# The drain of a two-layer block in another order: the roots, the transposes of x1 and the last sums moved on four engines

## The chip, the cores and the metric

One core of one Trainium2 chip. The time is the device time of one execution in microseconds (us), the median of several runs; lower is better. The kernel before took 449.24 us (three runs, 449.08 to 449.36).

## What is computed

The input x has 4096 tokens (8 sequences of 512) of 256 features, all fp32. Two stages follow each other, each with a residual and a layer norm without weights:

```python
def attn(x):                                  # retention with 4 heads
    q, k = rotary(x @ Wq, x @ Wk)             # 4 heads x 64
    v = x @ Wv                                # 4 heads x 128
    o = chunk_retention(q, k, v, gamma)       # decay gamma per head, running state per sequence
    o = rmsnorm(o, gn_weight) * silu(x @ Wg)
    return o @ Wo
def ffn(x):
    wg, wu, wd = (w_int / 127 for w_int in (w_gate, w_up, w_down))   # 256 -> 768 -> 256
    return (silu(x @ wg.T) * (x @ wu.T)) @ wd.T
x1 = layernorm(x + attn(x))
x2 = layernorm(x1 + ffn(x1))                  # the output
```

## The kernel before

The tokens are cut into 32 tiles of 128 (NT = 32, four to a sequence). Five engines each run an order of their own, written out by hand, and meet at counting semaphores. A *slot* s does each stage for another tile: the projections of tile s, the retention of tile s-1, the output product `attention_out` and the sum z1 of tile s-2, the first layer norm (x1) and its transpose of tile s-3, the gate and up products of the pair that holds tile s-4, the down product and the second sum z2 of tile s-6, and the second layer norm of tile s-7. The tiles of the feed-forward stage go in pairs (256 columns): an even slot makes blocks 0 to 2 of the hidden layer for the pair, the odd slot after it blocks 3 to 5. I write (t, j) for block j of the slot NT + t, so that (2, 0) to (3, 2) are the six blocks of the last pair, tiles 30 and 31.

fp32 products are made from parts: each operand is split in a high part (fp32r, written by ScalarE) and the low rest (a subtraction), and TensorE multiplies high by high, low by high and high by low. For integer weights the low part of the weight is nothing, and two products remain.

What follows the last full slot is the *drain*, slots 32 to 40, with its own order on every engine. The diff touches only this part:

- TensorE (PE), `drain` at L628. `turn_x1` (L471) transposes x1 of a tile into the bank b_state; it waits for x1 and until the tile before has been read out of the bank. `gate_up_block` (L525) is 8 matmuls. `down` (L563) comes in three parts (0, 1, 2), 4 matmuls each; part j needs the low parts of blocks j and 3+j of the pair, and part 0 also a free bank, named by `free`.
- For each block of the hidden layer a loop runs over two engines: ScalarE (ACT) takes the silu of the gate (`gate`, L800), VectorE (DVE) multiplies by up (`hidden`, L1016), ScalarE writes the high part (`split_h`, L813), and then it takes the silu of the next block. GpSimd (POOL) subtracts to get the low part (`split_h`, L1255). There are two buffers for a block.
- The layer norms: VectorE makes the sum (`residual_1`, L1099; `residual_2`, L1118), its statistics and their moments (`moments_1`, `moments_2`), GpSimd the inverse root (`inv_std_1`, `inv_std_2`, two small operations, L1287 and L1289), VectorE the scaled difference (`norm_1`, L1038; `norm_2`, L1050). x1 of a tile then goes through TensorE (L485), ScalarE (high part, L756) and VectorE (low part, `split_x1T`, L1074) before the gate product may read it. z1 and its moments have one buffer, z2 two.
- SyncE stores each finished tile (L360); it waits for `norm_2`.

A few lines show the two kinds of wait that matter here:

```python
pe.wait_ge(x1_ready, n + 1)        # turn_x1: x1 of tile n
pe.wait_ge(x1T_split, n)           # turn_x1 in the drain: tile n-1 read out of b_state
dve.wait_ge(x2_ready, n - 1)       # residual_2: tile n-2 has been normed (two buffers of z2)
```

Of the kernel before, what the change touches and what calls it, by code (L numbers as in the profile page):

```python
# [29 lines left out]
F32 = mybir.dt.float32  # L30
F32R = mybir.dt.float32r
I32 = mybir.dt.int32
ALU = mybir.AluOpType
# [18 lines left out]
FFN_LAG = 4  # L52
# [16 lines left out]
def build_block(nc, xT, x, w_proj, w_o, gn, w_ffn, rope, out):  # L69
    tokens = x.shape[0]  # L70
    NT = tokens // P
# [4 lines left out]
    with ExitStack() as ctx:  # L76
# [200 lines left out]
        def down_bank(s, t):  # L277

            if isinstance(s, int) and s >= NT - 1:
                return b_rows[(1, 0, 1, 0, 1, 0, 1)[s - NT + 1]]  # L280
            return row_bank(t + 1, 1)

        def x1_bank(s, t):
# [89 lines left out]
        def _(pe):  # L373
# [172 lines left out]
            def attention_out(s, q, t):  # L546

                n = s - 2
                if exists(n):
                    pe.wait_ge(yT_split, n + 1)  # L550
                    if is_slot(s, 2):
                        pe.wait_ge(wo_split, 1)
                    if without_down(s):
                        pe.wait_ge(rot_parts, s + 1)
                    elif is_slot(s, NT) or is_slot(s, NT + 1):
                        pe.wait_ge(z2_ready, s - DOWN_LAG)
                    else:
                        wait_bank(s, 4, row_stages)
                    stat = [(yT_hi[:, h * P:(h + 1) * P], yT_lo[:, h * P:(h + 1) * P]) for h in range(H)]
                    mov = [(wo_hi[:, h, :], wo_lo[:, h, :]) for h in range(H)]  # L560
                    split_product(wo_bank(s, t)[:, 0:D], stat, mov).then_inc(wo_done, 1)
# [66 lines left out]
            def drain(wide):  # L628

                q = NSEQ  # L630
                at = lambda t: (NT + t, q, t)
                update_state(*at(0))
                gate_up_block(*at(-1), 1, wide)
                down(*at(-1), wide, free=(z1_ready, NT - 2))
                gate_up_block(*at(-1), 2, wide)
                recall_and_score(*at(0))
                turn_x1(*at(0))
                turn_y(*at(0))
                down(*at(0), wide, (0, 1), free=(g_gated, NT))
                retain(*at(0))  # L640
                gate_up_block(*at(0), 0, wide)
                attention_out(*at(0))
                down(*at(0), wide, (2,))
                gate_up_block(*at(0), 1, wide)
                gate_up_block(*at(0), 2, wide)
                turn_y(*at(1))
                gate_up_block(*at(1), 0, wide)
                gate_up_block(*at(1), 1, wide)
                attention_out(*at(1))
                turn_x1(*at(1))  # L650
                gate_up_block(*at(1), 2, wide)
                down(*at(1), wide, free=(z1_ready, NT - 1))
                turn_x1(*at(2))
                down(*at(2), wide, free=(z1_ready, NT))
                gate_up_block(*at(2), 0, wide)
                gate_up_block(*at(2), 1, wide)
                down(*at(3), wide, (0,), free=(z2_ready, NT - 4))
                gate_up_block(*at(2), 2, wide)
                down(*at(3), wide, (1,))
                for j in range(3):  # L660
                    gate_up_block(*at(3), j, wide)
                down(*at(3), wide, (2,))
                down(*at(4), wide, (0, 1), free=(z2_ready, NT - 3))
                down(*at(5), wide, (0, 1), free=(z2_ready, NT - 2))
                down(*at(4), wide, (2,))
                down(*at(5), wide, (2,))

# [30 lines left out]
        def _(act):  # L698
# [201 lines left out]
            def drain():  # L900

                at = lambda t: (NT + t, NSEQ, t)
                mean_squares(*at(-1))
                keep_qk(*at(0))
                keep_state(*at(-1))
                gate(NT - 1, -1, 1)
                split_h(NT - 1, -1, 0)
                keep_x1(*at(0))
                split_h(NT - 1, -1, 1)
                gate(NT - 1, -1, 2)  # L910
                split_x1T(*at(0))
                split_y(*at(0))
                split_h(NT - 1, -1, 2)
                keep_x1(*at(1))
                mean_squares(*at(0))
                gate(NT, 0, 0)
                split_h(NT, 0, 0)
                gate(NT, 0, 1)
                gate(NT, 0, 2)
                split_h(NT, 0, 1)  # L920
                split_y(*at(1))
                split_h(NT, 0, 2)
                gate(NT + 1, 1, 0)
                split_h(NT + 1, 1, 0)
                gate(NT + 1, 1, 1)
                split_x1T(*at(1))
                split_h(NT + 1, 1, 1)
                keep_x1(*at(2))
                gate(NT + 1, 1, 2)
                split_h(NT + 1, 1, 2)  # L930
                split_x1T(*at(2))
                keep_x1(*at(3))
                for t in (2, 3):
                    for j in range(3):
                        gate(NT + t, t, j)
                        split_h(NT + t, t, j)
# [5 lines left out]
        def _(dve):  # L942
# [168 lines left out]
            def moments_1(n, waited=False):  # L1111

                if exists(n):
                    if not waited:
                        dve.wait_ge(z1_stats, n + 1)
                    dve.bn_aggr(mv1[:], st1[:]).then_inc(z1_moments, 1)  # L1116
# [23 lines left out]
            def slot(s, q, t):  # L1140
# [29 lines left out]
                if is_slot(s, FFN_LAG):  # L1170
                    tell_wide()

            def drain():

                at = lambda t: (NT + t, NSEQ, t)

                def sum_2(t):

                    residual_2(*at(t))
                    stats_2(*at(t))  # L1180
                    moments_2(NT + t - DOWN_LAG, back(NSEQ, t, DOWN_LAG)[1])

                norm_2(*at(-1))
                norm_1(*at(0))
                gated_output(*at(-1))
                hidden(NT - 1, -1, 1)
                sum_2(-1)
                hidden(NT - 1, -1, 2)
                mask(*at(0))
                split_x1T(*at(0))  # L1190
                split_y(*at(0))
                norm_2(*at(0))
                hidden(NT, 0, 0)
                residual_1(*at(0))
                gated_output(*at(0))
                hidden(NT, 0, 1)
                hidden(NT, 0, 2)
                residual_2(*at(0))
                split_y(*at(1))
                moments_1(NT - 2)  # L1200
                stats_2(*at(0))
                hidden(NT + 1, 1, 0)
                moments_2(NT - DOWN_LAG, back(NSEQ, 0, DOWN_LAG)[1])
                norm_1(*at(1))
                hidden(NT + 1, 1, 1)
                residual_1(*at(1))
                moments_1(NT - 1)
                split_x1T(*at(1))
                norm_2(*at(1))
                hidden(NT + 1, 1, 2)  # L1210
                norm_1(*at(2))
                sum_2(1)
                split_x1T(*at(2))
                sum_2(2)
                norm_2(*at(2))
                hidden(NT + 2, 2, 0)
                hidden(NT + 2, 2, 1)
                norm_2(*at(3))
                hidden(NT + 2, 2, 2)
                for j in range(3):  # L1220
                    hidden(NT + 3, 3, j)
                sum_2(3)
                sum_2(4)
                norm_2(*at(4))
                sum_2(5)
                norm_2(*at(5))
                norm_2(*at(6))
# [5 lines left out]
        def _(pool):  # L1233
# [90 lines left out]
            def drain():  # L1324

                at = lambda t: (NT + t, NSEQ, t)
                inv_std_1(*at(-1))
                rms_norm(*at(-1))
                split_h(NT - 1, -1, 0)
                split_h(NT - 1, -1, 1)  # L1330
                inv_std_2(*at(0))
                split_h(NT - 1, -1, 2)
                rms_norm(*at(0))
                split_h(NT, 0, 0)
                split_h(NT, 0, 1)
                split_h(NT, 0, 2)
                inv_std_1(*at(0))
                split_h(NT + 1, 1, 0)
                inv_std_2(*at(1))
                split_h(NT + 1, 1, 1)  # L1340
                inv_std_1(*at(1))
                split_h(NT + 1, 1, 2)
                inv_std_2(*at(2))
                inv_std_2(*at(3))
                for t in (2, 3):
                    for j in range(3):
                        split_h(NT + t, t, j)
                for t in (4, 5, 6):
                    inv_std_2(*at(t))

# [32 lines left out]
```

## Time and profile before

| | us |
|---|---|
| median of three runs | 449.24 |
| the profiled execution, own time | 449.29 |
| its span, first to last instruction | 447.6 |
| last matmul of the span starts | 441.01 |
| last operation of VectorE starts | 444.54 |
| granted TensorE clock, mean | 0.999 |

The span is the stretch from the first to the last instruction; the rest of the own time (1.7 us) lies around it. The views used are: the busy times of each engine (a busy engine is one that has an instruction in work); the chain of waits, which follows the work that ended last back in time; a table of busy time by stage; and the timeline of each engine in the last 30 us, which lists the start of each instruction, its duration, its source line and its tiles, and in brackets the idle time before it with what ended it. PE is a matmul, PEld the load of its weights.

### The profile page before, as it was taken

The numbers are of one execution on the slowest core, as the hardware profiler recorded it, in microseconds if no ns is written. First come the engines' busy times: TensorE is split into PE (matmuls) and PEld (weight loads), VectorE is DVE, ScalarE is ACT, GpSimd is POOL, SyncE is SP. The second block draws the span as 40 slices with busy tenths as digits, with TensorE's granted clock in tenths as the row PEclk, the third lists the DMA queues.
The fourth block names the chain that finished last, engine by engine and source line by source line (L and its number), as shares of the span: only waits on it lengthen the run. The fifth ranks groups of instructions, "written<-read, shape, count | busy, mean of one in ns | idle before, by whom it ended". The sixth has DMA issues, their size and how long they took to land.

```text
span 447.6 us, 10332 instructions
## 1 busy us (share of the span) xinstructions
PE 434.5 (97%) x3288; PEld 392.7 (88%) x3288; DVE 307.6 (69%) x785; ACT 269.3 (60%) x794; POOL 241.3 (54%) x381
## 2 busy tenths in 40 slices
PE   8989999999999999999999999999999999999994
PEld 3877889999999999999999999999999999999983
DVE  3989565677666677666768667577766667765774
ACT  5778766566655566654666556556665556665541
POOL 2654355655655466554666436665565536554564
PEclk9999999999999999999999999999999999999999
DMA  7911010010100101010010202002010100100011
GB/s 244 349 42 49 0 49 1 1 61 13 61 12 26 34 12 59 12 59 12 19 39 12 59 12 59 0 12 59 12 59 12 35 1 12 37 14 12 14 38 38
DMA packets 15932, 18.45 MB, mean 41 GB/s; under 512 B 1440, under 2 KB 13728, under 8 KB 15904
## 3 DMA queue, kind: packets, MB, share of 16 engines
q1 hardware_dynamic: 15904, 18.09, 12.7%
q8 instruction: 15, 0.25, 0.2%
q14 instruction: 13, 0.11, 0.1%
HBM read 13.89 MB, written 4.19 MB: 40 GB/s over the span
## 4 chain that ended last, share of the span: by engine, by line
PE 87%; DVE 6%; issue 2%; POOL 1%; ACT 1%; DMA 1%; SPq 0%; POOLq 0%; DVEq 0%; ACTq 0%
PE b_rows L399 44%; PE b_ffn L399 18%; PE b_head L496 6%; PE b_state L399 3%; PE b_head L464 3%; PE b_head L467 3%; PE b_turn L412 3%; PE b_turn L522 3%; PE b_ffn L485 2%; DMA wf_int<-in_w_proj 1%; DVE y L1095 1%; DVE qk L1012 1%; DVE rot_s L999 1%; POOL h_lo L1262 1%; DVE rot_c L992 1%
## 5 line engine op out<-in xcount | busy, mean ns | idle before, releaser
L1262 POOL TENSOR_TENSOR h_lo<-wf_int,h_hi 128x256 fp32r<-128x256 f32 x96 | 71.4, 743 | 61.4 <-ACT h_hi L822 61.0
L399 PE MATMUL b_ffn<-x1T_hi,wf_hi 128*128 128x256 f32 x384 | 92.7, 278 | 0.6 <-DVE x1T_lo L1074 0.6
L399 PE MATMUL b_ffn<-x1T_lo,wf_hi 128*128 128x256 f32 x384 | 91.8, 276 | 0.0
L399 PE MATMUL b_rows<-wp_hi,xT_hi 128*128 128x512 f32 x186 | 78.8, 424 | 0.0
L399 PEld LDWEIGHTS b_ffn<-x1T_hi,wf_hi 128*128 128x128 f32 x384 | 72.1, 188 | 3.9 <-DVE x1T_lo L1074 1.1
L399 PEld LDWEIGHTS b_ffn<-x1T_lo,wf_hi 128*128 128x128 f32 x384 | 72.1, 188 | 2.8
L1287 POOL TENSOR_TENSOR ve<-mv,eps 128x1 f32<-128x1 f32 x64 | 14.1, 221 | 111.7 <-DVE mv L1116 103.9
L399 PE MATMUL b_rows<-wp_hi,xT_lo 128*128 128x512 f32 x186 | 73.4, 395 | 0.0
L399 PE MATMUL b_rows<-wp_lo,xT_hi 128*128 128x512 f32 x186 | 73.3, 394 | 0.0
L786 ACT ACTIVATE sq<-b_head 128x128 f32<-128x128 f32 x124 | 34.5, 278 | 57.2 <-PE b_head L496 54.3
L1107 DVE TENSOR_TENSOR z<-b_rows,x_sb 128x256 f32<-128x256 f32 x32 | 13.6, 424 | 67.0 <-PE b_rows L399 67.0
L811 ACT ACTIVATE wf_int<-b_ffn 128x256 f32<-128x256 f32 x96 | 36.8, 384 | 27.2 <-PE b_ffn L399 27.1
L1028 DVE TENSOR_TENSOR wf_int<-b_ffn,wf_int 128x256 f32<-128x256 f32 x96 | 40.0, 417 | 17.0 <-ACT wf_int L811 14.0
L822 ACT CAST h_hi<-wf_int 128x256 fp32r<-128x256 f32 x96 | 38.9, 405 | 19.1 <-DVE wf_int L1028 19.1
L399 PE MATMUL b_rows<-wf_hi,h_hi 128*128 128x256 f32 x192 | 45.6, 278 | 0.3 <-POOL h_lo L1262 0.3
L399 PE MATMUL b_rows<-wf_hi,h_lo 128*128 128x256 f32 x192 | 45.3, 276 | 0.0
L1012 DVE TENSOR_TENSOR qk<-rot_c,rot_s 128x256 f32<-128x256 f32 x64 | 42.4, 701 | 3.9 <-DVE st L1134 2.9
L399 PEld LDWEIGHTS b_rows<-wp_hi,xT_lo 128*128 128x128 f32 x186 | 35.0, 188 | 8.5
L399 PEld LDWEIGHTS b_rows<-wp_hi,xT_hi 128*128 128x128 f32 x186 | 35.0, 188 | 4.4 <-ACT v_sb L735 0.2
L399 PEld LDWEIGHTS b_rows<-wp_lo,xT_hi 128*128 128x128 f32 x186 | 35.2, 189 | 4.1
L1289 POOL TENSOR_TENSOR rs<-ve,half_neg 128x1 f32<-128x1 f32 x64 | 34.9, 545 | 5.0
L399 PE MATMUL b_rows<-wo_hi,yT_hi 128*128 128x256 f32 x128 | 35.7, 279 | 1.1 <-DVE yT_lo L1083 1.1
(112 smaller groups left out, 1078.2 us busy)
## 6 DMA issues: line engine op xcount, KB each, us to landing
xT_raw<-in_xT SPq DMA_DIRECT2D x16, 256.0 KB, 3.1
x_sb<-in_x SPq DMA_DIRECT2D x16, 256.0 KB, 2.7
out<-wf_int SPq DMA_DIRECT2D x32, 128.0 KB, 1.7
wf_int<-in_w_ffn SPq DMA_DIRECT2D x6, 384.0 KB, 7.0
wf_int<-in_w_proj SPq DMA_DIRECT2D x6, 256.0 KB, 4.8
rope_sb<-in_rope SPq DMA_DIRECT2D x4, 256.0 KB, 6.6
wo_raw<-in_w_o SPq DMA_DIRECT2D x1, 512.0 KB, 7.6
gn_sb<-in_gn SPq DMA_DIRECT2D x1, 0.5 KB, 7.0
```

Source lines behind the costliest of these rows:

```text
L399: mm = pe.matmul(dst, a, b, start=(i == 0 and j == 0 and not begun), stop=(i == n - 1 and j == len(passes) - 1 and not more), skip_group_c ...
L412: mm = pe.transpose(b_turn[:, b * P:(b + 1) * P], qk[:, t % 2, b * P:(b + 1) * P], ident[:])
L496: mm = pe.matmul(o_of(n, h), attn[:, h, :], v_sb[:, tn % 2, h * DV:(h + 1) * DV], start=False, stop=True, skip_group_check=True)
L786: act.activation(sq[:], o_of(n, h), ACT.Square, scale=float(DV) ** -0.5, accum_out=ms[:, tn % 2, h:h + 1]).then_inc(squared, 1)
L811: act.activation(act_g[:, u], b_ffn[u][:, 0:256], ACT.Silu, scale=SCALE).then_inc(silu_done[j], 1)
L822: act.copy(h_hi[:, ((t - FFN_LAG) // 2) % 2, hb], h_full[:, u]).then_inc(h_high[j], 1)
L1012: last = dve.tensor_tensor(halves(qk[:, t % 2])[:, :, e], halves(rot_c[:])[:, :, e], halves(rot_s[:])[:, :, e], sign)
L1028: dve.tensor_tensor(h_full[:, u], b_ffn[u][:, 256:512], act_g[:, u], ALU.mult).then_inc(h_ready[j], 1)
L1107: dve.tensor_tensor(z1[:], wo_bank(s, t)[:, 0:D], x_sb[:, tn, :], ALU.add).then_inc(z1_ready, 1)
L1262: pool.tensor_tensor(h_lo[:, ring, hb], h_full[:, u], h_hi[:, ring, hb].bitcast(F32), ALU.subtract).then_inc(h_split[j], 1)
L1287: pool.tensor_tensor(ve, mv[:, 1:2], eps[:, 0:1], ALU.add).then_inc(var, 1)
L1289: pool.tensor_tensor(rs, ve, half_neg[:, 0:1], ALU.pow).then_inc(rstd, 1)
```

## The change

Only the order in the drain changes, with two subtractions that go from GpSimd to VectorE and one bank. No work is added or left out.

- TensorE: (1, 2) is computed ahead of the transpose of x1 of tile 30. The transpose of tile 31 comes later, behind the first part of the down product of tile 28. Parts of the down products of tiles 29, 30 and 31 are spread otherwise, and tile 31 takes the bank b_head0 in place of a bank of b_rows, free once y is ready.
- ScalarE: the silu of (1, 2) ahead of the high part of x1T of tile 30.
- VectorE: the moments of z1 of tile 30 ahead of the product (0, 1), x1 of tile 30 ahead of the product (1, 0), the sum z1 of tile 31 with its statistics ahead of the product (1, 1); the low part of x1T of tile 30 and x2 of tile 26 behind x1 of tile 31. The sum of tile 29 moves in front of (3, 1), x2 of tile 29 in front of the sum of tile 30. VectorE now makes the low parts of (3, 1) and (3, 2).
- GpSimd: the root for x1 of tile 30 ahead of the low parts of (0, 1) and (0, 2), the root for x2 of tile 26 behind the one for x1 of tile 31, and no more low parts of (3, 1) and (3, 2).

```diff
@@ down_bank @@
             if isinstance(s, int) and s >= NT - 1:
-                return b_rows[(1, 0, 1, 0, 1, 0, 1)[s - NT + 1]]
+                return b_head[0] if s == LAST - 3 else b_rows[(1, 0, 1, 0, 1, 0)[s - NT + 1]]
@@ TensorE, drain @@
                 attention_out(*at(1))
+                gate_up_block(*at(1), 2, wide)
                 turn_x1(*at(1))
-                gate_up_block(*at(1), 2, wide)
                 down(*at(1), wide, free=(z1_ready, NT - 1))
+                down(*at(2), wide, (0,), free=(z1_ready, NT))
                 turn_x1(*at(2))
-                down(*at(2), wide, free=(z1_ready, NT))
+                down(*at(2), wide, (1, 2))
+                down(*at(3), wide, (0,), free=(z2_ready, NT - 4))
                 gate_up_block(*at(2), 0, wide)
                 gate_up_block(*at(2), 1, wide)
-                down(*at(3), wide, (0,), free=(z2_ready, NT - 4))
+                down(*at(3), wide, (1,))
                 gate_up_block(*at(2), 2, wide)
-                down(*at(3), wide, (1,))
-                for j in range(3):
-                    gate_up_block(*at(3), j, wide)
+                gate_up_block(*at(3), 0, wide)
                 down(*at(3), wide, (2,))
-                down(*at(4), wide, (0, 1), free=(z2_ready, NT - 3))
-                down(*at(5), wide, (0, 1), free=(z2_ready, NT - 2))
+                gate_up_block(*at(3), 1, wide)
+                gate_up_block(*at(3), 2, wide)
+                down(*at(4), wide, (0,), free=(z2_ready, NT - 3))
+                down(*at(5), wide, (0,), free=(y_ready, NT))
+                down(*at(4), wide, (1,))
+                down(*at(5), wide, (1,))
                 down(*at(4), wide, (2,))
                 down(*at(5), wide, (2,))
@@ ScalarE, drain @@
                 gate(NT + 1, 1, 1)
+                split_h(NT + 1, 1, 1)
+                gate(NT + 1, 1, 2)
                 split_x1T(*at(1))
-                split_h(NT + 1, 1, 1)
+                split_h(NT + 1, 1, 2)
                 keep_x1(*at(2))
-                gate(NT + 1, 1, 2)
-                split_h(NT + 1, 1, 2)
                 split_x1T(*at(2))
@@ VectorE: a low part of h, new @@
+            def split_h(s, t, j):
+                u, hb, ring = (3 * t + j) % 2, 3 * (t % 2) + j, ((t - FFN_LAG) // 2) % 2
+                dve.wait_ge(h_high[j], s - FFN_LAG + 1)
+                dve.tensor_tensor(h_lo[:, ring, hb], h_full[:, u], h_hi[:, ring, hb].bitcast(F32),
+                                  ALU.subtract).then_inc(h_split[j], 1)
@@ VectorE, drain @@
                 gated_output(*at(0))
+                moments_1(NT - 2)
                 hidden(NT, 0, 1)
                 hidden(NT, 0, 2)
                 residual_2(*at(0))
                 split_y(*at(1))
-                moments_1(NT - 2)
+                norm_1(*at(1))
                 stats_2(*at(0))
                 hidden(NT + 1, 1, 0)
                 moments_2(NT - DOWN_LAG, back(NSEQ, 0, DOWN_LAG)[1])
-                norm_1(*at(1))
+                residual_1(*at(1))
                 hidden(NT + 1, 1, 1)
-                residual_1(*at(1))
                 moments_1(NT - 1)
+                hidden(NT + 1, 1, 2)
+                norm_1(*at(2))
                 split_x1T(*at(1))
                 norm_2(*at(1))
-                hidden(NT + 1, 1, 2)
-                norm_1(*at(2))
                 sum_2(1)
                 split_x1T(*at(2))
                 sum_2(2)
...
                 hidden(NT + 2, 2, 2)
-                for j in range(3):
-                    hidden(NT + 3, 3, j)
+                hidden(NT + 3, 3, 0)
                 sum_2(3)
+                hidden(NT + 3, 3, 1)
+                split_h(NT + 3, 3, 1)
+                hidden(NT + 3, 3, 2)
+                split_h(NT + 3, 3, 2)
+                norm_2(*at(4))
                 sum_2(4)
-                norm_2(*at(4))
                 sum_2(5)
@@ GpSimd, drain @@
                 split_h(NT, 0, 0)
+                inv_std_1(*at(0))
                 split_h(NT, 0, 1)
                 split_h(NT, 0, 2)
-                inv_std_1(*at(0))
                 split_h(NT + 1, 1, 0)
-                inv_std_2(*at(1))
                 split_h(NT + 1, 1, 1)
                 inv_std_1(*at(1))
+                inv_std_2(*at(1))
                 split_h(NT + 1, 1, 2)
                 inv_std_2(*at(2))
                 inv_std_2(*at(3))
-                for t in (2, 3):
-                    for j in range(3):
-                        split_h(NT + t, t, j)
+                for j in range(3):
+                    split_h(NT + 2, 2, j)
+                split_h(NT + 3, 3, 0)
```

## Rows read from the trace of the kernel before

**Rows 1.** Page, first part: busy time, share of the span, instructions.
```profile
PE 434.5 (97%) x3288; PEld 392.7 (88%) x3288; DVE 307.6 (69%) x785; ACT 269.3 (60%) x794; POOL 241.3 (54%) x381
```
**Rows 2.** Busy time by stage: stretch, its length, each engine (count), clock, DMA.
```profile
425.00:430.00 5.00, 4.03 (x34) 3.63 (x33) 4.49 (x13) 2.25 (x7) 3.58 (x7) 1.00 0.08 26
```
**Rows 3.** Chain of waits, the last 6 us: start, duration, what.
```profile
441.89 0.41 DVE wf_int L1050
442.43 0.43 DVE wo_raw L1126
...
444.54 0.41 DVE wf_int L1050
```
**Rows 4.** Timeline of TensorE, matmuls: start, duration, operation, [idle before, releaser].
```profile
424.97 0.28 PE L399 MATMUL b_rows<-wo_hi,yT_lo 128*128 128x256 f32 x1
425.72 0.44 PE L485 MATMUL b_state<-ident,x 128*128 128x128 f32 x2 [0.48 <-DVE x L1038]
...
429.01 0.44 PE L485 MATMUL b_state<-ident,x 128*128 128x128 f32 x2 [0.49 <-DVE x L1038]
429.20 0.36 PE L399 MATMUL b_rows<-wf_hi,h_hi 128*128 128x256 f32 x1
429.40 0.28 PE L399 MATMUL b_rows<-wf_hi,h_lo 128*128 128x256 f32 x1
...
430.67 0.28 PE L399 MATMUL b_ffn<-x1T_hi,wf_hi 128*128 128x256 f32 x1
...
440.56 0.28 PE L399 MATMUL b_rows<-wf_hi,h_lo 128*128 128x256 f32 x1
```
**Rows 5.** Timeline of VectorE.
```profile
420.10 1.11 DVE L1095 SCALAR_TENSOR_TENSOR y<-b_head,rms,g_sb 128x128 f32<-128x128 f32 x4
...
424.75 0.92 DVE L1038 TENSOR_SCALAR x<-z,mv,rs 128x256 f32<-128x256 f32 x1 [0.39 <-POOL rs L1289]
...
425.92 0.41 DVE L1107 TENSOR_TENSOR z<-b_rows,x_sb 128x256 f32<-128x256 f32 x1
426.36 0.43 DVE L1109 BATCH_NORM_STATS2 st<-z 128x6 f32<-128x256 f32 x1
...
428.54 0.41 DVE L1038 TENSOR_SCALAR x<-z,mv,rs 128x256 f32<-128x256 f32 x1 [0.37 <-POOL rs L1289]
428.87 0.42 DVE L1126 SCALAR_TENSOR_TENSOR wo_raw<-b_rows,wf_int 128x256 f32<-128x256 f32 x1
...
429.89 0.42 DVE L1074 TENSOR_TENSOR x1T_lo<-b_state,x1T_hi 128x256 fp32r<-128x256 f32 x1
...
440.87 0.42 DVE L1126 SCALAR_TENSOR_TENSOR wo_raw<-b_rows,wf_int 128x256 f32<-128x256 f32 x1 [1.25 <-PE b_rows L399]
```
**Rows 6.** Timeline of ScalarE: silu, high part, next silu, and the last silu.
```profile
431.78 0.38 ACT L811 ACTIVATE wf_int<-b_ffn 128x256 f32<-128x256 f32 x1 [1.62 <-PE b_ffn L399]
432.66 0.41 ACT L822 CAST h_hi<-wf_int 128x256 fp32r<-128x256 f32 x1 [0.50 <-DVE wf_int L1028]
432.97 0.38 ACT L811 ACTIVATE wf_int<-b_ffn 128x256 f32<-128x256 f32 x1
...
437.77 0.38 ACT L811 ACTIVATE wf_int<-b_ffn 128x256 f32<-128x256 f32 x1
```
**Rows 7.** Timeline of GpSimd: three low parts and tile 31's root.
```profile
424.78 0.73 POOL L1262 TENSOR_TENSOR h_lo<-wf_int,h_hi 128x256 fp32r<-128x256 f32 x1
...
427.65 0.23 POOL L1287 TENSOR_TENSOR ve<-mv,eps 128x1 f32<-128x1 f32 x1
427.96 0.55 POOL L1289 TENSOR_TENSOR rs<-ve,half_neg 128x1 f32<-128x1 f32 x1
428.68 0.86 POOL L1262 TENSOR_TENSOR h_lo<-wf_int,h_hi 128x256 fp32r<-128x256 f32 x1 [0.18 <-ACT h_hi L822]
...
439.13 0.74 POOL L1262 TENSOR_TENSOR h_lo<-wf_int,h_hi 128x256 fp32r<-128x256 f32 x1 [0.45 <-ACT h_hi L822]
```
**Rows 8.** Line L1012 of VectorE: count, duration ns min/median/max, first and last start.
```profile
L1012 DVE TENSOR_TENSOR qk<-rot_c,rot_s x64: 410/652/1134, 12.6 to 401.3; 128x256 f32<-128x256 f32 x64
```

## Prediction

> **What bounds the kernel now.** I read the page first: TensorE is busy for 97% of the span [rows 1], so up to the drain only its work counts, and the diff doesn't touch that. Then the busy time by stage: of the last stages before the tail it is 425 to 430 us where TensorE is short of full, 4.03 of 5 us, while VectorE has 4.49 [rows 2]. The timeline of TensorE names the two holes: 0.48 us and 0.49 us of idle, each ahead of a transpose of x1 (tile 30 at 425.72, tile 31 at 429.01), each ended by VectorE's x1 [rows 4]. From 430.67 the six blocks of the last pair run. There TensorE is not the limit: the silu of one block starts 1.19 us after the one before (431.78, 432.97), its high part at +0.88 [rows 6], while 8 matmuls at (430.67 - 429.40) / 11 = 0.1155 us take 0.92 [rows 4]. That loop of ScalarE and VectorE sets the last silu, 437.77, and with GpSimd's low part (439.13 + 0.74 = 439.87) [rows 6, 7] the earliest last down parts; TensorE gets to the one of tile 30 at 440.56 less three matmuls, 440.21, 0.3 us later, so both are close. Last, the chain of waits: the sum of tile 30 starts at 440.87 [rows 5], x2 of tile 29 at 441.89 stands before the sum of tile 31, at 442.43, and x2 of tile 31 starts at 444.54 [rows 3].
>
> What the end follows is thus: x1 of tile 31, its transpose, the low part of x1T, six loops, two down parts, the tail. I walk this in the new order, with the times of the profiled execution (span 447.6, own time 449.29, 0.05 over the median). Handovers are read off pairs of rows: matmul start to the engine that reads it 0.31 (440.56 to 440.87), silu to silu 1.19, high part to GpSimd's low part 0.48 (437.77 + 0.88 to 439.13), a VectorE operation of 256 elements behind another 0.33 (428.54 to 428.87), a sum with its statistics and moments 1.02 (428.87 to 429.89) [rows 4 to 7].
>
> **Tile 30's root and x1: the first hole goes.** VectorE's moments now stand behind y (420.10, four operations, 1.02 until the next), so at 421.12; GpSimd's root (two operations, 0.31 apart, and 0.55 for the second [rows 7]; 0.26 to hand over, an estimate between the 0.31 and the 0.05 of the other handovers) is done at 422.2, before the low part of (0, 1). x1 of tile 30 is wanted at 425.99 and waits only for its turn on VectorE, a slack of over 3 us that even a repeat of the 0.92 leaves open; the product (1, 0) behind it slips to about 424.3, and (1, 2) may start from 424.8. So TensorE goes from 424.97 straight on: (1, 2) until 425.99, transpose, 12 matmuls of tile 27 by the same form as 429.01 to 430.67, 1.66 us, until 427.65, and 4 more of tile 28 until 428.1 [rows 4, 5].
>
> **Tile 31's root: nothing is won.** The sum z1 of tile 31 needs the output product, last matmul 424.97, so 425.28 in place of 425.92, 0.64 sooner; statistics 425.73 (425.92 to 426.36 is 0.44), then the product (1, 1) at 426.04. This product stood ahead of the sum (425.59 by the +0.84 behind 424.75) and now stands behind it: 0.45 later. Moments follow at 426.36. But on GpSimd the low part of (1, 1) still stands ahead of that root, and it needs the product and the high part: 426.04 + 0.45 (0.88 less the 0.43 from silu to product, its 0.38 and a handover of 0.05) + 0.48 = 426.97, then 0.69 and 0.28 (427.65 and 427.96 are 0.31 apart): root at 427.94, x1 0.58 behind it (427.96 to 428.54) at 428.52 against 428.54 [rows 5 to 7]. So the second hole stays: TensorE is out of work at 428.1, not 428.35, and waits longer.
>
> **The transposes of tiles 30 and 31 come closer together.** The low part of x1T of tile 30 now stands behind x1 of tile 31 on VectorE: 428.85, done 429.27. The transpose of tile 31 waits for it (one bank): 429.32 in place of 429.01, +0.31. Behind it stand 12 matmuls as before, which would put (2, 0) at 430.98.
>
> **Low part of tile 31: the step that costs.** Before, VectorE had only the sum of tile 27 between x1 of tile 31 and this low part: 428.54 to 429.89. Now it has three: the low part of tile 30 (0.33), x2 of tile 26, and the sum. x2 of tile 26 waits for a root that GpSimd starts only behind tile 31's: root done at 427.94 + 0.55 = 428.49, the next two 0.06 + 0.35 (0.31 in the rows, a little more beside x1) and 0.55: 429.45, so x2 starts at 429.48. GpSimd's low part of (1, 2) starts 0.03 later. The same pair stands in the trace: x1 at 424.75, low part at 424.78, and x1 took 0.92 instead of 0.41, while GpSimd took its usual 0.73; where VectorE was 0.14 ahead (428.54 and 428.68), it kept 0.41 and GpSimd took 0.86 [rows 5, 7]. 0.03 is nearer to 0.03: I take 0.92, the other end 0.41. Sum of tile 27 at 429.48 + 0.84 = 430.32, low part of tile 31 at 431.34, done 431.75; (2, 0) starts at 431.8 against 430.67: **+1.13**. As TensorE now comes out of a wait, its second matmul has the gap 0.20 (429.20 to 429.40) in place of 0.1155: the first silu of the pair is at 433.0 against 431.78, +1.24 [rows 4 to 6].
>
> The Trainium skill says of this port, in "SBUF — State Buffer", section "SBUF: two separate sides", that VectorE in a two-port mode and GpSimd hold it for a whole instruction and that the one which starts first gets it. The trace agrees with the lock (0.92 is 0.41 and most of a 0.73), not with the order at 424.75. By the rule x2 of tile 26 would keep 0.41; that is the second case below.
>
> **The six loops.** Nothing in their period changes, 1.19 each: silus at 433.0, 434.2, 435.4, 436.6, 437.8. TensorE feeds each in time (only two down parts of 4 matmuls, 0.46 each, lie between the six blocks of 0.92). One thing is new: the sum of tile 29 (1.02) is put ahead of the product (3, 1). Product (3, 0) at 437.02, sum 437.36 to 438.37; the product (3, 1) was due at 438.21: +0.16. Last silu 439.13.
>
> **Low parts of (3, 1) and (3, 2) on VectorE.** 128x256 from two SBUF tensors: 0.41 at least by the 64 of L1012, 1.13 at most beside GpSimd [rows 8]. GpSimd's part takes 0.74. After the high part it is 0.43 + 0.41 = 0.84 against 0.48 + 0.74 = 1.22 [rows 7]. I take 0.41: at its second one GpSimd has nothing left to do. The first (439.25) puts (3, 2)'s product at 439.59, not 439.55. High part 440.04, low part 440.47 to 440.88; down part 2 of tile 30 at 440.93 against 440.21. Its fourth matmul starts 0.20 + 2 x 0.1155 = 0.43 later, the sum of tile 30 0.31 behind that, at 441.67 against 440.87: **+0.80**. TensorE has until then done the other down parts, in the wait.
>
> **The tail.** x2 of tile 29 is now ahead of the sum of tile 30, in the wait for TensorE (440.8 to 441.2). Then sum 30, sum 31 (+1.02), moments, x2 of tile 31 at 1.20 + 0.92 behind the start of sum 31 (442.43 to 444.54 is 2.11). Before, 440.87 to 444.54 was 3.67; now 1.02 + 2.11 = 3.13: **-0.54** [rows 3, 5]. The bank b_head0 has been free since the end of y, 420.10 + 1.11 [rows 5], and stores keep their order; both cost nothing, as SyncE's last store follows x2 of tile 31 in either kernel.
>
> **Sum.** 0.80 - 0.54 = +0.26 us: 449.29 + 0.26 = 449.55 for a run like the profiled one, 449.5 against the median of 449.24.
>
> **Rivals.** Second case: VectorE wins the port at 429.48 (0.51 less on VectorE; then 12 matmuls with GpSimd's part until 430.4 put (2, 0) at 431.5): 0.34 less, 449.2. For it: the 428.54 pair. Against it: the 424.75 pair, whose distance is the same.
> Third case, faster: the root of tile 26 or x1 of tile 31 comes early enough that VectorE is never last, and only the order of TensorE counts: (2, 0) at 430.98, +0.31, all else as above: 0.82 less, 448.7. If also nothing in the loops slips (0.16), 448.5. It needs the high part of (1, 1) 0.7 us sooner than I have it, and (1, 1) waits for a sum that waits for a matmul at 424.97.
> Fourth case, slower: the low parts on VectorE meet GpSimd's root for tile 29 (about 438.9 to 439.5) and go as L1012's slow ones. It decides when the first low part starts inside that root. With 0.74 for each instead of 0.41 the product (3, 2) and the last part slip by 0.33 each: 450.2; with the median of L1012, 0.65, 450.0. Against it: only two small operations of one element per partition run there.
> That the change does not do what it says: the first hole must go, as its cause is an order in two queues; if it stayed, x1 of tile 30 would be late by another wait, and 0.5 us came on top of the first case, 450.0.
>
> **How the numbers follow.** First case 0.50, second 0.18, third 0.14, fourth and the last together 0.18. No change is what lies within 0.2% (0.9 us), which is what a measurement of this kernel can tell. The first two are inside it, the third inside for more than half (its 448.7 and 448.5 are 0.5 and 0.7 below; an error of a few tenths in my handovers puts a part outside), the fourth at its edge. Faster 0.11, same 0.74, slower 0.15. Range 448.4 to 450.2: the third case's lower end at one side, the fourth's price at the other.
>
> **What would show it.** The idle ahead of the transpose of tile 30 is gone. x1 of tile 31 starts within 0.2 of 428.5. TensorE's idle before the transpose of tile 31 is over 1 us. x2 of tile 26 takes 0.9 us, or 0.4 and the second case holds. The first silu of the last pair is near 433.0. From the sum of tile 30 to x2 of tile 31 it is 3.1 us. The prediction is wrong in kind if x1 of tile 31 starts before 428, or if (2, 0) starts before 431.

## The result and the profile after

The changed kernel takes 450.04 us against 449.31 us before (medians of 17 runs each), a ratio of 1.0017 with a 95% interval of 1.001 to 1.0025: +0.7 us, slower, and by less than the 0.9 us that the prediction called no change. The prediction had 449.5 us, +0.26. The changed kernel's profiled execution has a span of 448.7 us and an own time of 450.39 us.

First the timeline of VectorE after, as in [rows 5]. Here all is 0.57 us late already at the first sum z1 of the drain (419.86, before 419.29), where the two programs are still the same; so times are best read from that sum on.

```profile
419.86 0.42 DVE L1111 TENSOR_TENSOR z<-b_rows,x_sb 128x256 f32<-128x256 f32 x1
...
424.03 0.63 DVE L1042 TENSOR_SCALAR x<-z,mv,rs 128x256 f32<-128x256 f32 x1
...
425.85 0.42 DVE L1111 TENSOR_TENSOR z<-b_rows,x_sb 128x256 f32<-128x256 f32 x1 [0.44 <-PE b_rows L399]
...
429.12 0.41 DVE L1042 TENSOR_SCALAR x<-z,mv,rs 128x256 f32<-128x256 f32 x1 [0.88 <-POOL rs L1303]
429.45 0.42 DVE L1078 TENSOR_TENSOR x1T_lo<-b_state,x1T_hi 128x256 fp32r<-128x256 f32 x1
429.96 0.82 DVE L1054 TENSOR_SCALAR wf_int<-wo_raw,mv,rs 128x256 f32<-128x256 f32 x1
430.70 0.41 DVE L1130 SCALAR_TENSOR_TENSOR wo_raw<-b_rows,wf_int 128x256 f32<-128x256 f32 x1
...
431.71 0.39 DVE L1078 TENSOR_TENSOR x1T_lo<-b_state,x1T_hi 128x256 fp32r<-128x256 f32 x1
...
439.57 0.42 DVE L1181 TENSOR_TENSOR h_lo<-wf_int,h_hi 128x256 fp32r<-128x256 f32 x1 [0.47 <-ACT h_hi L826]
...
442.07 0.42 DVE L1130 SCALAR_TENSOR_TENSOR wo_raw<-b_rows,wf_int 128x256 f32<-128x256 f32 x1 [0.52 <-PE b_rows L399]
...
445.22 0.42 DVE L1054 TENSOR_SCALAR wf_int<-wo_raw,mv,rs 128x256 f32<-128x256 f32 x1 [0.70 <-POOL rs L1303]
```

x1 of tile 31 (429.12) has not moved: 9.26 us behind the first sum, before 9.25. Behind it stand the low part of tile 30, x2 of tile 26 with 0.82 us, the sum, and only then the low part of tile 31.

GpSimd after, the stretch behind tile 31's root, as in [rows 7]:

```profile
427.57 0.74 POOL L1276 TENSOR_TENSOR h_lo<-wf_int,h_hi 128x256 fp32r<-128x256 f32 x1 [1.00 <-ACT h_hi L826]
428.27 0.19 POOL L1301 TENSOR_TENSOR ve<-mv,eps 128x1 f32<-128x1 f32 x1
428.54 0.54 POOL L1303 TENSOR_TENSOR rs<-ve,half_neg 128x1 f32<-128x1 f32 x1
429.05 0.19 POOL L1301 TENSOR_TENSOR ve<-mv,eps 128x1 f32<-128x1 f32 x1
429.31 0.61 POOL L1303 TENSOR_TENSOR rs<-ve,half_neg 128x1 f32<-128x1 f32 x1
429.90 0.73 POOL L1276 TENSOR_TENSOR h_lo<-wf_int,h_hi 128x256 fp32r<-128x256 f32 x1
```

The low part of (1, 2) starts at 429.90, 0.06 ahead of x2 of tile 26, and ends at 430.63; x2 ends 0.15 later. TensorE after, the two transposes and (2, 0), as in [rows 4]; an idle time before an operation stands in brackets:

```profile
426.56 0.38 PE L485 MATMUL b_state<-ident,x 128*128 128x128 f32 x2
...
430.01 0.41 PE L485 MATMUL b_state<-ident,x 128*128 128x128 f32 x2 [1.24 <-DVE x1T_lo L1078]
...
432.15 0.39 PE L399 MATMUL b_ffn<-x1T_hi,wf_hi 128*128 128x256 f32 x1 [0.25 <-DVE x1T_lo L1078]
```

The idle ahead of the transpose of tile 30 is gone, the one ahead of tile 31's has grown from 0.49 to 1.24, and there is a new one before (2, 0). The chain of waits after shows the stretch ahead of x2 of tile 26 as one line of handovers, from the high part of (1, 1) to the roots of tiles 31 and 26:

```profile
427.09 0.41 ACT h_hi L826
427.51 0.07 issue
427.57 0.74 POOL h_lo L1276
428.32 0.16 POOL ve L1301
428.48 0.07 issue
428.54 0.54 POOL rs L1303
429.08 0.16 POOL ve L1301
429.25 0.07 issue
429.31 0.62 POOL rs L1303
```

Last, the store of tile 31. Of the executions' own time, a part lies behind the start of x2 of tile 31: before 449.29 - 444.54 = 4.75 us, after 450.39 - 445.22 = 5.17. The issues of L360 in the last stretch, first before, then after, show what differs, the landing (the time from issue until all of the store has arrived):

```profile
L360 SPq DMA_DIRECT2D out<-wf_int x1: 332/332/332, 445.0 to 445.0; - x1
DMA to landing us min/median/max: 2.1/2.1/2.1
```
```profile
L360 SPq DMA_DIRECT2D out<-wf_int x1: 332/332/332, 445.7 to 445.7; - x1
DMA to landing us min/median/max: 2.5/2.5/2.5
```

What is late is a small part of it. The bytes moved in steps of 0.1 us, from 1.0 us behind the start of x2 of tile 31 on, before and after:

```profile
GB/s 10 10 61 266 379 348 205 51 20 31 10 0 0 0 0 0 0 0 0 0 0 0 0 0 0 0 0 0 0 0 0 0 0 0 0 0 0 0 0 0
```
```profile
GB/s 0 0 61 266 358 358 195 31 10 10 10 21 31 20 20 0 0 0 0 0 0 0 0 0 0 0 0 0 0 0 0 0 0 0 0 0 0 0 0 0
```

Most has moved in the first eight steps in either kernel; behind it comes a trail of a few packets, for three steps before and for seven after.

### The profile page after: what moved, and what is told of

Same layout as the page of the kernel before. It is cut to its first block, busy times and chain, and to the rows that moved or that the text cites. A ratio compares the mean times of both kernels' runs of the same rounds, so it can differ in the third digit from the quotient of the medians.

```text
span 448.7 us, 10332 instructions
## 1 busy us (share of the span) xinstructions
PE 434.5 (97%) x3288; PEld 393.0 (88%) x3288; DVE 308.9 (69%) x787; ACT 268.9 (60%) x794; POOL 238.6 (53%) x379
## 4 chain that ended last, share of the span: by engine, by line
PE 88%; DVE 6%; issue 2%; DMA 1%; POOL 1%; ACT 1%; SPq 0%; POOLq 0%; DVEq 0%; ACTq 0%
PE b_rows L399 44%; PE b_ffn L399 19%; PE b_head L496 6%; PE b_state L399 3%; PE b_head L464 3%; PE b_head L467 3%; PE b_turn L412 3%; PE b_turn L522 3%; PE b_ffn L485 2%; DMA wf_int<-in_w_proj 1%; DVE y L1099 1%; DVE qk L1016 1%; DVE rot_s L1003 1%; DVE rot_c L996 1%; DVE attn L1068 1%
## 5 line engine op out<-in xcount | busy, mean ns | idle before, releaser
L1276 POOL TENSOR_TENSOR h_lo<-wf_int,h_hi 128x256 fp32r<-128x256 f32 x94 | 69.2, 736 | 60.8 <-ACT h_hi L826 60.1
L399 PE MATMUL b_rows<-wf_hi,h_hi 128*128 128x256 f32 x186 | 44.5, 279 | 0.1
L399 PE MATMUL b_rows<-wf_hi,h_lo 128*128 128x256 f32 x186 | 44.1, 277 | 0.0
```

Source lines behind the costliest of these rows:

```text
L399: mm = pe.matmul(dst, a, b, start=(i == 0 and j == 0 and not begun), stop=(i == n - 1 and j == len(passes) - 1 and not more), skip_group_c ...
L1276: pool.tensor_tensor(h_lo[:, ring, hb], h_full[:, u], h_hi[:, ring, hb].bitcast(F32), ALU.subtract).then_inc(h_split[j], 1)
```

## The experiments

In all of them I read three numbers from the profile: S, where the first sum z1 of the drain (tile 30) starts; D, from there to the start of x2 of tile 31; T, the own time less that start. Before: S 419.29, D 25.25, T 4.75. After: 419.86, 25.36, 5.17. Where a profile is meant, it is one execution; the ratio is to the kernel before on the same chip, with its 95% interval.

**The kernel before, unchanged.** No edit.

> The kernel before, unchanged, as a measure of how far two labels of one program stand apart. Theory A (the changed kernel loses about 0.1 us in the drain, the rest of its 0.7 us is how the loads at the start happened to land, as in the profile, where all is 0.57 us late before the first changed instruction): ratio 1.0000 within 0.0008, and the time of the first sum z1 scatters by some tenths from execution to execution. Theory B (the changed program starts later each time, by its layout): the same here, since the program is the same; the two part in the next run.

449.21 us, ratio 0.9994 (0.998 to 1.0007). S 419.26, D 25.49, T 4.43. D is 0.24 more than in the first profile of the same program, and 0.15 of that arises between two products of the last pair, (2, 2) and (3, 0). A difference in D of 0.1 or 0.2 between the two kernels is thus not told from none.

**The changed kernel again.** No edit.

> The changed kernel once more. Theory A: 0.1 to 0.4 us over the kernel before on the same chip (ratio 1.0002 to 1.0009), the drain from the first sum z1 of tile 30 to x2 of tile 31 25.4 us as in its first profile (25.25 before). Theory B: again 0.6 to 0.8 us (1.0013 to 1.0018), and the first sum z1 again near 30.1 us instead of 29.5.

449.74 us, ratio 1.0001 (0.9989 to 1.0013): here the interval does not tell it from the kernel before. It is 0.53 us over the unchanged kernel above and 0.29 over the median of all 35 runs of the kernel before on this chip. S 419.46, D 25.35, T 4.92. D is the same to 0.01 us; S is not late again (first sum z1 of the program 29.6, not 30.1). Over all 14 profiles S lies between 418.74 and 419.86, mean 419.19 in the three with the old order and 419.35 in the eleven with the new one. Theory B, a later start by layout, is not borne out. Of theory A, the changed kernel's drain of 25.4 us holds, but a loss of 0.1 us in it does not: D of the kernel before is now 25.25 and 25.49, mean 25.37, so D of the two kernels is the same as far as two profiles each can tell. Chance at the start does not carry the rest: T is high again.

**x2 of tile 29 ahead of the sum of tile 30, alone, in the kernel before.**

```diff
                 sum_2(3)
+                norm_2(*at(4))
                 sum_2(4)
-                norm_2(*at(4))
```

> The kernel before with one edit: x2 of tile 29 ahead of the sum of tile 30. By my walk x2 of tile 29 goes in the wait for TensorE, and the sum of tile 31 to x2 of tile 31 moves up: from the sum of tile 30 to x2 of tile 31 3.13 us instead of 3.67, time 0.5 us less (ratio 0.9988). Rival: x2 of tile 29 in front only pushes the sum of tile 30 later by its 0.4 us, the gain is under 0.2 us.

449.01 us, ratio 0.9987 (0.997 to 1.0003): not told from no change. The profile tells: D 24.85, 0.40 and 0.64 under the two profiles of the kernel before. The sum of tile 30 stands behind x2 of tile 29, which waits for its root; it is 0.13 later than in the first profile and 0.12 sooner than in the second:

```profile
440.39 0.41 DVE L1050 TENSOR_SCALAR wf_int<-wo_raw,mv,rs 128x256 f32<-128x256 f32 x1 [1.05 <-POOL rs L1289]
440.72 0.41 DVE L1126 SCALAR_TENSOR_TENSOR wo_raw<-b_rows,wf_int 128x256 f32<-128x256 f32 x1
```

From the sum of tile 30 on it is 3.14 us (3.67 before): the term of 0.54 stands, and the rival, a gain under 0.2, is refuted. T is 4.96.

**x2 of tile 26 later, in the changed kernel.**

```diff
                 split_x1T(*at(1))
-                norm_2(*at(1))
                 sum_2(1)
                 split_x1T(*at(2))
+                norm_2(*at(1))
                 sum_2(2)
```

> The changed kernel with one edit on VectorE: x2 of tile 26 behind the low part of x1T of tile 31. By my walk x2 of tile 26 (it waits for its root and then for the port) holds back that low part, so the last pair starts at about 431.0 on the prediction's clock instead of 431.6: 0.5 to 0.8 us less than the changed kernel, x2 of tile 31 earlier by as much. Rival: VectorE is not what (2, 0) waits for, the transposed tile or the down parts come as late, and the time stays as the changed kernel's within 0.2 us.

449.32 us, ratio 0.9995 (0.9983 to 1.0007), 0.42 under the changed kernel on the same chip. D 24.82, -0.53: the low end of what was expected, and the wait for VectorE before (2, 0) is gone. The step is confirmed: x2 of tile 26 held the last pair back.

**Tile 31's root sooner, in the changed kernel.**

```diff
-                split_h(NT + 1, 1, 1)
                 inv_std_1(*at(1))
+                split_h(NT + 1, 1, 1)
                 inv_std_2(*at(1))
                 split_h(NT + 1, 1, 2)
```

> The changed kernel with one edit on GpSimd: the root for x1 of tile 31 ahead of the low part of (1, 1). By my walk x1 of tile 31 starts 0.8 to 0.9 us sooner, the transpose of tile 31 too, but x2 of tile 26 still stands ahead of the sum of tile 27 and of the low part of x1T, with its root now behind a low part: (2, 0) only 0.3 us sooner, so 0.2 to 0.4 us less than the changed kernel. Rival: the root was what held everything, the gain is the full 0.8 us.

449.61 us, ratio 0.9999 (0.9988 to 1.0009). x1 of tile 31 comes 0.97 us sooner (8.29 behind the first sum), its transpose 0.64, x2 of tile 31 only 0.38: D 24.98. Alone, the root is mostly swallowed by x2 of tile 26, as expected.

**Both edits**, and the root of tile 26 behind the low part of (1, 2).

```diff
@@ GpSimd @@
+                inv_std_1(*at(1))
                 split_h(NT + 1, 1, 1)
-                inv_std_1(*at(1))
-                inv_std_2(*at(1))
                 split_h(NT + 1, 1, 2)
+                inv_std_2(*at(1))
@@ VectorE @@
-                norm_2(*at(1))
                 sum_2(1)
                 split_x1T(*at(2))
+                norm_2(*at(1))
```

> The changed kernel with both edits, and on GpSimd also the root of tile 26 behind the low part of (1, 2). By my walk the transpose of tile 31 comes 1.0 us sooner and nothing of VectorE stands before its low part: TensorE alone sets (2, 0), 1.4 to 1.5 us sooner than in the changed kernel, and the loops carry it to the end: from the sum z1 of tile 30 to x2 of tile 31 about 23.9 us (25.35 in the changed kernel, 25.25 to 25.5 before), ratio to the kernel before 0.997 to 0.998. Rival: another step takes the wait over (down parts of tile 28 that need the low part of (1, 2)), and less than 1 us comes.

448.92 us, ratio 0.9984 (0.9973 to 0.9995): faster than the kernel before, with an interval that leaves out 1; the changed kernel has 1.0017 and 1.0001. D 24.14, 1.22 less than the changed kernel, 0.24 short of my 23.9. VectorE shows where the 0.24 is: x1 of tile 31 now meets two low parts on GpSimd and takes 0.73, and the transpose still waits 0.54 for the low part of tile 30.

```profile
427.32 0.73 DVE L1042 TENSOR_SCALAR x<-z,mv,rs 128x256 f32<-128x256 f32 x1
427.98 0.41 DVE L1078 TENSOR_TENSOR x1T_lo<-b_state,x1T_hi 128x256 fp32r<-128x256 f32 x1
```

**The low parts of (3, 1) and (3, 2) back on GpSimd, in the changed kernel.**

```diff
@@ VectorE @@
-                split_h(NT + 3, 3, 1)
-                split_h(NT + 3, 3, 2)
@@ GpSimd @@
-                split_h(NT + 3, 3, 0)
+                for j in range(3):
+                    split_h(NT + 3, 3, j)
```

> The changed kernel with the low parts of (3, 1) and (3, 2) back on GpSimd. By my walk that costs 0.3 to 0.4 us at the last low part (1.22 us behind the high part, not 0.84), less the 0.1 us that the first one takes from VectorE: 0.2 to 0.4 us more than the changed kernel. Rival: TensorE or VectorE sets the end anyway, no difference.

450.72 us, ratio 1.0023 (1.001 to 1.0036). D 25.97, +0.61, more than the 0.2 to 0.4 expected. I had left out that tile 29's root then stands behind these low parts, and x2 of tile 29 ahead of the sum of tile 30:

```profile
442.34 0.41 DVE L1054 TENSOR_SCALAR wf_int<-wo_raw,mv,rs 128x256 f32<-128x256 f32 x1 [2.06 <-POOL rs L1301]
442.67 0.42 DVE L1130 SCALAR_TENSOR_TENSOR wo_raw<-b_rows,wf_int 128x256 f32<-128x256 f32 x1
```

So the move to VectorE is worth 0.6 us in this order; the two edits belong together.

**x2 of tile 29 back behind the sum of tile 30, in the changed kernel.**

```diff
-                norm_2(*at(4))
                 sum_2(4)
+                norm_2(*at(4))
```

> The changed kernel with x2 of tile 29 back behind the sum of tile 30. From the sum of tile 30 to x2 of tile 31 3.67 us again instead of 3.13. Theory C (the last store lands later in the changed kernel since the store of tile 29 goes out earlier and apart from the others; own time less the start of x2 of tile 31 was 4.4 and 4.75 us in two profiles of the kernel before, 4.9 to 5.2 in four with x2 of tile 29 moved up): that remainder falls to 4.4 to 4.8, and the time stays within 0.2 us of the changed kernel. Theory D (the remainder has to do with something else): it stays at 4.9 to 5.2 and the time is 0.5 us more.

450.18 us, ratio 1.001 (1.0 to 1.002). D 25.85, +0.50, and T 4.53, with a landing of 1.9 us. That is what theory C expected of both: what D loses, T gives back, and the time is near the changed kernel's. But C also names a cause, the early store of tile 29; two others, the queue and the idle time of the DMA engines, are tried first, then this one.

**The last store on ScalarE's queue**, in the kernel with both edits and in the changed kernel.

```diff
@@ SyncE, slot @@
-                if exists(n):
+                if exists(n) and not is_slot(s, LAST - 1):
@@ ScalarE, at the end of the drain @@
+                act.wait_ge(x2_ready, NT)
+                act.dma_start(out[(NT - 1) * P:NT * P, :], x2[:, (NT - 1) % 2, :]).then_inc(stored[(NT - 1) % 2], 16)
```

> The kernel of the two edits together (x2 of tile 26 later, both roots sooner) with one more edit: the last store, of tile 31, goes out on ScalarE's queue and not on SyncE's. If the late landing of the last store has to do with what is queued ahead of it on SyncE's queue, the remainder (own time less the start of x2 of tile 31) falls from 4.9 to 4.5 us or less and the time by 0.4 us. If it has to do with the DMA engines, it stays at 4.8 to 5.3 us. The drain from the sum z1 of tile 30 to x2 of tile 31 stays at 24.1 us.

> The changed kernel with the last store on ScalarE's queue. The same two readings as for the run before: remainder at or under 4.6 us if SyncE's queue is the cause, 4.9 to 5.5 us if the DMA engines are; drain 25.35 us in either case.

With both edits: 448.41 us, ratio 0.9978 (0.9969 to 0.9987), the fastest kernel of the study; D 24.08, T 4.96. The changed kernel: 449.88 us, ratio 1.0013 (1.0004 to 1.0023); D 25.34, T 5.37. T stays: SyncE's queue is not the cause. D and T of the first are those of the kernel with both edits within 0.06 us, so its better ratio is no gain of the store; the two intervals overlap.

**A load between the stores, in the changed kernel.**

```diff
+        again = sem("again")
...
+                    if s == LAST - 3:
+                        sp.wait_ge(z1_ready, NT)
+                        sp.wait_ge(z2_ready, NT - 1)
+                        sp.dma_start(x_sb[:, 0, :], x[0:P, :]).then_inc(again, 16)
+                sp.wait_ge(again, 16)
```

> The changed kernel with one more transfer, a load of 128 KB into a buffer that nothing reads any more, issued at the sum of tile 30, so between the stores of tiles 29 and 30. The theory that the last stores land late because the DMA engines have been idle since the early store of tile 29 expects the last landing back at 1.7 to 2.1 us and a remainder of 4.4 to 4.75 us, 0.4 us less in time. If how long they were idle is not the cause, the landing stays at 2.3 to 2.8 us, or grows by what the load delays.

449.85 us, ratio 1.0015 (1.0006 to 1.0024). D 25.34, T 5.00, landing 2.3 us: not the idle time.

**The store of tile 29 held back, in the changed kernel.**

```diff
                 for s in range(NT, LAST):
+                    if s == LAST - 3:
+                        sp.wait_ge(z2_ready, NT - 1)
                     slot(s, s // TS, s % TS)
```

> The changed kernel with the store of tile 29 held back on SyncE until the sum of tile 30 is done: 0.9 us later, 2.7 us ahead of x2 of tile 31 (3.6 in the changed kernel, 2.2 in the kernel before). The computation is the same, drain 25.35 us. If the early store of tile 29 is what makes the last store land late, its landing falls from 2.3 to 2.8 us to 1.7 to 2.1 us, the remainder (own time less the start of x2 of tile 31) from 4.9 to 5.2 us to 4.4 to 4.75 us, and the time by 0.3 to 0.5 us. If the store of tile 29 has no part in it, all three stay.

449.92 us, ratio 1.0008 (0.9997 to 1.0018). D 25.34, T 5.17, landing 2.5 us: nothing changed. The store of tile 29 went out 2.7 us ahead of x2 of tile 31, against 3.6 in the changed kernel and 2.2 in the kernel before, so 0.9 of the 1.4 us by which it goes out earlier are not the cause; the other 0.5 was not tried.

## Why the prediction came out right, and where it was short

Times behind the first sum z1 of the drain, after less before:

| step | predicted | measured |
|---|---|---|
| x1 of tile 31 | -0.02 | +0.01 |
| transpose of tile 31 | +0.31 | +0.43 |
| low part of tile 31 | +1.45 | +1.25 |
| (2, 0) on TensorE | +1.13 | +0.91 |
| last silu | +1.36 | +1.11 |
| sum of tile 30 | +0.80 | +0.63 |
| from there to x2 of tile 31 | -0.54 | -0.52 |
| sum, D | +0.26 | +0.11 (-0.02 with the mean of two profiles each) |
| behind x2 of tile 31, T | 0 | +0.42 (this pair of profiles) |

**Tile 30 and tile 31.** The first hole went, and tile 31's root won nothing, for the reason given: the low part of (1, 1), now later, stands before it. TensorE's idle of 1.24 us is the "over 1 us".

**The costly step.** The mechanism was right and its size 0.2 us too high, in two halves. x2 of tile 26 started 0.09 sooner on the prediction's clock (429.96 - 0.57 = 429.39, not 429.48): the two operations of its root lie 0.26 apart, not 0.35. And it took 0.82, not 0.92, because GpSimd started 0.06 ahead of it, not 0.03 behind: with nothing to wait for, GpSimd starts an operation 0.02 or 0.03 ahead of the stamped end of the one before (429.05 against 428.54 + 0.54, 429.90 against 429.31 + 0.61), where the walk had 0.06 behind. The second case did not come. That the change loses there and is not bound by TensorE was then shown by moving x2 of tile 26. One slip of the walk stands beside it: 1.13 and the 0.085 of the wider gap make 1.21 at the first silu, not 1.24.

**Loops and the low parts on VectorE.** The product (3, 1) was held by the sum of tile 29 as said (438.69, with the silu at 438.19 + 0.43 = 438.62, so by 0.07, not 0.16), and the two low parts took 0.42 and 0.43: the fourth case is refuted. What I did not see is that moving them also frees tile 29's root: with them back on GpSimd, D is 0.61 more.

**The step that failed: "both cost nothing, as SyncE's last store follows x2 of tile 31 in either kernel".** It follows, but it lands later. T was 4.43, 4.53 and 4.75 us in the three profiles with x2 of tile 29 behind the sum of tile 30 (both of the kernel before, and the changed kernel with that edit undone), landing 1.8 to 2.1 us; in the eleven with x2 of tile 29 ahead it was 4.90 to 5.57, mean 5.16, landing 2.2 to 2.8. So the term put at nothing was about 0.5 us: the five profiles of the changed order on the computing engines have a mean T of 5.13, the two of the kernel before 4.59. With D the same, that is the +0.5 that the five ratios of this order average to (1.0017, 1.0001, 1.0013, 1.0015, 1.0008, mean 1.0011); the 0.7 of the first measurement is the highest of them.

How well it is shown that T goes with this one edit: undoing it in the changed kernel brought T down clear of those five profiles (4.53 against 4.92 to 5.37), and the time stayed (ratio 1.001) though D grew by 0.5. Adding it to the kernel before gave 4.96, over 4.75 and 4.43, but the ratio there, 0.9987, is too wide to say whether the gain was given back. These are single profiles; the split of 3 against 11 is without overlap, but its edges, 4.75 and 4.90, are closer than two profiles of one program.

**What no experiment varied.** In every profile the DMA view has two transfers of 16 KB each of another queue, q8, kind "instruction", among the last stores. The second one, before (window 444.45 to 444.55) and after (445.15 to 445.25); the last number is its time as a share of 16 engines over the 0.1 us of the window:

```profile
q8 instruction: 1, 0.02, 65.2%
```
```profile
q8 instruction: 1, 0.02, 89.8%
```

So it took 0.652 x 16 x 0.1 = 1.04 us before and 1.44 after. If the view places a transfer by its start, which I take it to do, it ended 1.0 and 1.4 us behind the start of x2 of tile 31. Worked out in the same way for all profiles, that end lies 0.6 to 1.0 us behind in the three with low T and 1.2 to 2.0 in the other eleven, and in the main T rises with it: 4.43 and 4.53 at 0.7 and 0.6, 5.53 and 5.57 at 2.0 and 1.75. The store of tile 29 shows the same. Where the first transfer began 1.0 us or more ahead of its issue (again the three), it landed in 1.7 us; 0.3 ahead, in 1.9 to 2.2 (three profiles); 0.6 to 1.3 behind, in 2.7 to 3.4 (eight). In the kernel before, the six stores that land in 2.1 us or more each have such a transfer within 1 us of their issue. The likely cause of the late landing is thus a meeting of a store with one of these transfers, and the edit on VectorE changes which of them meet. No run moved the transfers alone, so this is not shown, and what starts them stays open. SyncE's queue, idle time of the DMA engines and the early store of tile 29 were tried and are not it, the last within the limit said there.

**The chances.** The first case, no change with a small loss, is what came; the measured 0.7 us lay at the slow side of it by a term that no case had. That it stayed inside is in part luck: the walk of D was 0.15 to 0.3 us too slow, which made up for a part of T, and the range reached to 450.2 only by the price of the fourth case, which did not come. The chances also do not quite add up: the third case had 0.14, more than half of it inside no change, which leaves under 0.07 for faster, and 0.11 was given.

## What to carry to other kernels

When an order written by hand is changed, write down for each queue what is now late next: an operation put behind a later one (x2 of tile 26 behind tile 31's root) can hold everything that stands behind it. A low part, a root and the operation that waits for the root belong in one consideration; moving one of them alone won 0.4 or 0.5 us, all together 1.2. A gain at the last store must be read to the end of the execution, not to the last instruction of an engine, and where a store lands late, the DMA view should be read for transfers that the program did not issue. And one more profile of the kernel before tells what a difference of 0.1 us in the drain is worth.

## What the runs showed of the hardware that I had not expected

- The last store of 128 KB lands in 1.8 to 2.8 us, where the median of all stores is 1.7, and which it is goes with an edit on VectorE 4 us earlier (3 profiles against 11). The lateness is a trail of a few packets, and it goes with the end of a 16 KB transfer of kind "instruction" that took 0.9 to 1.6 us in the 14 profiles; that it is the cause is not shown.
- An operation of VectorE that met a low part of GpSimd's ended about 0.15 us behind it in each case that I read (430.63 and 430.78 here). The Trainium skill, "SBUF — State Buffer", section "SBUF: two separate sides", has the first to start win: here the trace agrees, GpSimd being 0.06 ahead; at 424.75 in the kernel before VectorE is stamped 0.03 ahead and lost, and so it did in two more profiles of that order (424.71 against 424.75, 424.46 against 424.50).
- Up to the first sum z1 of the drain all 14 programs have the same order, and S spreads over 1.1 us; D repeats to 0.02 us in five profiles of the changed order on the computing engines (25.34 to 25.36), and to 0.24 in the two of the kernel before.
